# Flamingo block on one core: the first layer's network on sorted tokens instead of on all experts

## The reference, cut to what matters

```python
logits = gelu(xf @ router_w1 + router_b1) @ router_w2 + router_b2
topk_p, topk_i = top_k(softmax(logits), 2)          # shares normalised to 1
v, integrated = 0, xf
for _ in range(2):
    ctx = concat([integrated, v])
    shared_ctrl = gelu(ctx @ shared_w1 + shared_b1) @ shared_w2 + shared_b2
    x_sh, v_sh = inl(shared_ctrl, integrated, v, mu)
    ctrl = expert(ctx, topk_i)                      # its own network for each choice
    x_r, v_r = inl(ctrl, ...) weighted by topk_p and summed over the two choices
    x_next, v_next = sw * (x_sh, v_sh) + (1 - sw) * (x_r, v_r)
    halt = sigmoid(gelu(integrated @ halt_w1 + halt_b1) @ halt_w2 + halt_b2)
    integrated += halt * (x_next - integrated)
    v += halt * (v_next - v)
out = xf + integration_weight * (gelu(integrated @ refine_w1 + b) @ refine_w2 + b)

def inl(ctrl, xs, vs, mu):
    a, b, g = split(ctrl, 3)
    v_next = sigmoid(a) * vs - softplus(b) * (xs - mu)
    return xs + 0.1 * sigmoid(g) * v_next, v_next
```

## Time and profile before

| | us |
|---|---|
| median of 3 runs (lowest to highest) | 648.78 (643.36 to 662.13) |
| the profiled execution | 646.05 |
| its span, first to last instruction | 644.2 |
| mean granted clock of TensorE | 0.928 of full |

### The profile page before, as it was taken

One profiled execution on the slowest core, in us unless ns is written; L12 is line 12 of the kernel. 1 busy time (PEld: TensorE's weight loads), 2 busy tenths in 40 slices (PEclk: granted clock), 3 DMA queues, 4 the chain that ended last, 5 costly groups with the idle time before them and its releaser, 6 DMA issues.

```text
span 644.2 us, 9928 instructions
## 1 busy us (share of the span) xinstructions
PE 572.7 (89%) x3318; PEld 336.9 (52%) x3318; DVE 424.6 (66%) x1054; ACT 308.8 (48%) x630; POOL 203.5 (32%) x214
## 2 busy tenths in 40 slices
PE   4777999999998898999999999998864499999994
PEld 2432344444453343444444444465554499999993
DVE  3897778887277799777335766768757354545445
ACT  2553466666658744554343535455441144444431
POOL 3829301010034360003790500012564623333331
...
GB/s 276 147 197 131 100 187 12 4 2 3 1 193 355 79 1 1 1 0 0 1 130 0 2 14 1 2 0 6 29 35 194 99 214 283 327 327 308 343 211 205
DMA packets 48198, 71.14 MB, mean 110 GB/s; under 512 B 11420, under 2 KB 35300, under 8 KB 47860
## 3 DMA queue, kind: packets, MB, share of 16 engines
...
## 4 chain that ended last, share of the span: by engine, by line
PE 62%; DVE 10%; SPq 10%; DMA 6%; issue 5%; ACT 4%; another core or an unknown queue 2%; POOL 1%; DVEq 0%; ACTq 0%; POOLq 0%
PE psum L1943 18%; PE psum L1758 6%; PE psum L1745 5%; PE psum L1888 5%; PE psum L2219 4%; PE psum L1766 3%; DMA wb<-in_wall_dram 3%; PE psum L1890 3%; PE psum L1722 3%; PE psum L2230 2%; PE psum L1940 2%; SPq L592 2%; DMA stacked<-parts 2%; DMA stacks<-maxT 1%
## 5 line engine op out<-in xcount | busy, mean ns | idle before, releaser
L1943 PE MATMUL psum<-hidden,ew 128*128 128x512 f32 x320 | 145.3, 597 | 0.0
L856 ACT ACTIVATE probs<-psum 128x512 f32<-128x512 f32 x128 | 74.7, 598 | 55.4 <-PE psum L1745 54.9
L1943 PEld LDWEIGHTS psum<-hidden,ew 128*128 128x128 f32 x320 | 61.5, 192 | 69.7 <-issue 68.3
L1136 DVE TENSOR_REDUCE negmax<-psum 128x4 f32<-128x1024 f32 x64 | 76.9, 1211 | 17.8 <-PE psum L1722 17.2
L2219 PE MATMUL psum<-xbT,wb 128*128 128x128 f32 x624 | 79.9, 283 | 1.8 <-DMA wb<-in_wall_dram 1.5
L1652 DVE SCALAR_TENSOR_TENSOR gated<-psum,wb,silu_g 128x128 f32<-128x128 f32 x156 | 43.9, 343 | 55.9 <-ACT silu_g L1056 50.6
L1056 ACT ACTIVATE silu_g<-psum,wb 128x128 f32<-128x128 f32 x156 | 44.6, 370 | 70.6 <-PE psum L2219 52.7
L2219 PEld LDWEIGHTS psum<-xbT,wb 128*128 128x128 f32 x624 | 76.1, 199 | 2.9 <-DMA wb<-in_wall_dram 2.3
L799 POOL DMA_INDIRECT sorted_y<-yb,xb x39 | 37.4, 958 | 80.1 <-DVE yb L1644 80.1
L1745 PE MATMUL psum<-stacks 50*128 50x256 bf16 x256 | 52.6, 298 | 6.2 <-DMA stacks<-maxT 4.0
L2230 PE MATMUL psum<-wb,gated 128*128 128x128 f32 x312 | 42.3, 279 | 8.6 <-DVE gated L1652 8.3
...
## 6 DMA issues: line engine op xcount, KB each, us to landing
...
sorted_x<-in_slots_dram SPq DMA_DIRECT2D x1, 9815.0 KB, 32.7
...
back<-sorted_y SPq DMA_DIRECT2D x4, 512.0 KB, 5.4
...
```

The source lines that it names most:

```text
L856: nc.scalar.activation(probs[:, g % 2, h % 4, :, :], s2[n % 2].rearrange("p (k q) -> p k q", k=2), ACT.Exp, scale=float(HD) ** -0.5).then_ ...
L1136: nc.vector.tensor_reduce(negmax[:, p].rearrange("p h q -> p (h q)"), psum[:, i:i + 2, :].rearrange("p h (q k) -> p (h q) k", q=2), AX.X, ...
L1943: last = nc.tensor.matmul(dst, ew2[:, j, cols], hidden[:, c, k - 1, j, :], start=False, stop=(j == 3))
```

## The change

The first layer's network now computes each expert only for the tokens that chose it. Tokens are sorted in two halves of 1024. A half has 2048 rows (two choices) in regions packed to multiples of 128: 23 blocks (`FIRST_BLOCKS`), each with one expert, whose weights SP loads by a value from `first_table`. All elementwise work is in rows (tokens on partitions). A group is up to four blocks, or one chunk for the shared network; a sub-stage (`subs`) has three routed groups (12 or 11 blocks, `PIECES`), in step 1 with two shared groups ahead of them in every first piece; sub-stage 0 has the four shared groups of step 0. On every engine the sub-stages run in order: `units_of` (transposes, first matmul, gelu), then softplus, then sigmoids, then shares.

States go through DRAM: `scatter_rows` sends normalised tokens to `first_x`, `store_shares` (SP) writes each group's shares, `gather_shares` brings them home by token, `combine` adds them up, `scatter_states` sends the new states to `first_xv` for step 1. `final_columns` turns the last state for `refine_up`. The second layer's chain for chunks 0 and 1 starts after the last group. The masks, their spreading and the columns' state are gone; the constants fall from 25 DMAs to 17. The old functions named in the section above (`hidden_unit`, `spread_choice`, `mask_first`, `controller`, `gate_parts`, `first_step`, `second_step`) and their calls are taken away. `slots` is set, and the new buffers are cleared, by ScalarE's queue within attention (`CLEAR_AT`). `X_BUFS` falls from 10 to 8, and `back` lies over `xp`. The core of the added lines:

```diff
+CLEAR_AT = {(2, 13): "slots", (4, 5): "first_x", (5, 5): "first_xv"}
...
+W_BUFS, X_BUFS = 4, 8
...
+HALVES = 2
+HC = NC // HALVES
+FIRST_BLOCKS = (2 * HC * CH + E * (P - 1)) // P
+HALF_ROWS = FIRST_BLOCKS * P
+FIRST_THRESHOLDS = HC * CH // P
+PIECES = ((0, 12), (12, FIRST_BLOCKS))
+GATHER = 4
+W1_V, W1_OUT, W1_B = HID, 2 * HID, 2 * HID + 3 * D
+W1_COLS = W1_B + 1
+W1_BUFS = 16
+SOFT_BUFS, SIG_BUFS = 3, 4
...
+        add_sub([("shared", 0, c, 4) for c in range(NC)])
+        for it in range(2):
+            for half in range(HALVES):
+                for i, (j0, j1) in enumerate(PIECES):
+                    members = [("shared", 1, HC * half + c, 4) for c in range(HC)] if it and i == 0 else []
+                    add_sub(members + [("routed", it, (half, j), min(GATHER, j1 - j)) for j in range(j0, j1, GATHER)])
...
+            def load_first_rows(it, half, i):
+                j0, j1 = PIECES[i]
+                if it == 0:
+                    sp.wait_ge(rows_out[half], 16 * HC * GR)
+                else:
+                    sp.wait_ge(rows_out[half], 16 * 2 * HC * GR)
+                if it or half:
+                    was = groups_of(*((it, 0) if half else (it - 1, 1)), i)
+                    sp.wait_ge(share_done, was[-1] + 1)
+                if it == 0:
+                    sp.dma_start(xr[:, j0:j1, 1, :], sorted_rows(first_x, half, j0, j1 - j0)).then_inc(rows_in[i], 16)
+                else:
+                    sp.dma_start(xr[:, j0:j1, :, :].rearrange("p j a f -> p j (a f)"),
+                                 sorted_rows(first_xv, half, j0, j1 - j0)).then_inc(rows_in[i], 16)
+            def store_shares(g):
+                _, it, (half, j), n = groups[g]
+                sp.wait_ge(share_done, g + 1)
+                if it == 0:
+                    out_of, dst = rc[:, j:j + n, :, :].rearrange("p j a f -> p j (a f)"), first_c
+                else:
+                    out_of, dst = rc[:, j:j + n, 1, :], first_d
+                sp.dma_start(sorted_rows(dst, half, j, n), out_of).then_inc(shares_out[piece_of(g)], 16)
...
+            def gather_shares(it, c):
+                half = c // HC
+                for i in range(len(PIECES)):
+                    pool.wait_ge(shares_out[i], stored_shares(it, half, i))
+                if it or c >= 2:
+                    pool.wait_ge(combined, NC * it + c - 1)
+                src, n = (first_d, D) if it else (first_c, 2 * D)
+                for t in range(TC):
+                    for k in range(2):
+                        at = 2 * (c * TC + t) + k
+                        nc.gpsimd.indirect_dma_start(brought[:, c % 2, t, k, 0:n], None, src[half],
+                                                     bass.IndirectOffsetOnAxis(ap=slot1[:, at:at + 1], axis=0)).then_inc(home_in[c % 2], 16)
...
+            for half in range(HALVES):
+                for c in range(HC * half, HC * half + HC):
+                    exp_of_gap(c)
+                for c in range(HC * half, HC * half + HC):
+                    scatter_rows(c)
             for c in range(NC):
+                plain_sum(c)
+            for half in range(HALVES):
+                for c in range(HC * half, HC * half + HC):
+                    gather_shares(0, c)
+                for c in range(HC * half, HC * half + HC):
+                    scatter_states(c)
             for c in range(NC):
+                gather_shares(1, c)
+            pool.wait_ge(share_done, len(groups))
             rstd_of_chunk(2, 0)
             rstd_of_chunk(3, 0)
             rstd_of_chunk(2, 1)
...
+            def clear(which):
+                if which == "slots":
+                    act.dma_start(sorted_x.rearrange("(a b) f -> a (b f)", a=16 * (SLOTS // P)),
+                                  a["slots"].rearrange("(a b) f -> a (b f)", a=16 * (SLOTS // P))).then_inc(slots_cleared, 16)
+                    return
+                dst, n = (first_x, D) if which == "first_x" else (first_xv, 2 * D)
+                act.wait_ge(prepared, 1)
+                for half in range(HALVES):
+                    act.dma_start(dst[half].rearrange("(p j) f -> p j f", p=P),
+                                  zeros[:, 0:n].rearrange("p (o f) -> p o f", o=1).to_broadcast([P, FIRST_BLOCKS, n])).then_inc(first_cleared, 16)
...
+            def first_gelus(g):
+                act.wait_ge(up_psum, g + 1)
+                ps = bank[2 + g % 2]
+                if not is_routed[g]:
+                    nc.scalar.activation(shared_h[0:96, groups[g][2], :], ps[0:96, :], ACT.Gelu, bias=sb1[:, 0:1]).then_inc(gelu_done, 1)
+                    return
+                _, _, (_, j), n = groups[g]
+                for i in range(n):
+                    last = nc.scalar.activation(routed_h[0:HID, (j // GATHER) % 3, i * P:(i + 1) * P], ps[0:HID, i * P:(i + 1) * P], ACT.Gelu,
+                                                bias=w1[0:HID, (first_weight(g) + i) % W1_BUFS, W1_B:W1_B + 1])
+                last.then_inc(gelu_done, 1)
...
+            def units_of(sub):
+                for i, g in enumerate(sub):
+                    if g in turned:
+                        keep_turned(g)
+                    if i:
+                        first_gelus(sub[i - 1])
+                first_gelus(sub[-1])
+            def gates_of(sub):
+                nc.scalar.preload_act_table_set("natural_log_exp_and_others")
+                for g in sub:
+                    softplus(g)
+                for g in sub:
+                    sigmoids(g)
...
+            def give_share(g):
+                steps.wait()
+                if not step_of[g]:
+                    nc.vector.scalar_tensor_tensor(x_share(g), v_share(g), DT, gate(g, "g"), ALU.mult, ALU.mult).then_inc(share_done, 1)
+                    return
+                at = groups[g][2]
+                if is_routed[g]:
+                    v = t = tiles_of(xr, g, 0)
+                else:
+                    v, t = xv[:, TC * at:TC * at + TC, 0, :], x_share(g)
+                steps.then(nc.vector.tensor_tensor(t, v, gate(g, "a"), ALU.mult))
+                steps.wait()
+                steps.then(nc.vector.tensor_tensor(t, t, difference(g), ALU.subtract))
+                steps.wait()
+                stored(g)
+                nc.vector.scalar_tensor_tensor(x_share(g), t, DT, gate(g, "g"), ALU.mult, ALU.mult).then_inc(share_done, 1)
...
+            COMBINE_AFTER = {3: (0, 0), 4: (0, 1), 5: (0, 2), 6: (0, 3), 7: (1, 0), 8: (1, 1)}
+            for i, sub in enumerate(subs):
+                if i:
+                    units_of(sub)
+                    softplus_of(sub)
+                    shares_of(sub)
+                if i in COMBINE_AFTER:
+                    combine(*COMBINE_AFTER[i])
...
+            add_refined(0)
+            layer_norm_apply(0, turn(2, 0))
+            maxima2(0)
+            maxima2(1)
+            sums_of(0)
+            fuse(0)
+            fuse(1)
+            third_stats(0)
+            layer_norm_rows(0)
+            add_refined(1)
+            layer_norm_apply(1, turn(2, 1))
+            choose(0)
+            combine(1, 2)
+            maxima2(2)
+            maxima2(3)
+            weights_of(0)
+            slots_of(0)
+            combine(1, L)
...
+            def product(g, part):
+                kind, _, at, n = groups[g]
+                m = products.index((g, part))
+                if m >= 3:
+                    pe.wait_ge(*part_read(m - 3))
+                pe.wait_ge(gelu_done, g + 1)
+                dst = part_bank(m)
+                for i in range(n):
+                    if kind == "shared":
+                        h = shared_h[0:97, at, i * P:(i + 1) * P]
+                        if part == "halt":
+                            last = nc.tensor.matmul(dst[:, i:i + 1], h, sw2[0:97, 3 * D:3 * D + 1], start=True, stop=True)
+                            continue
+                        w = sw2[0:97, 0:3 * D]
+                    else:
+                        h = routed_h[0:HID + 1, (at[1] // GATHER) % 3, i * P:(i + 1) * P]
+                        w = w1[0:HID + 1, (first_weight(g) + i) % W1_BUFS, W1_OUT:W1_OUT + 3 * D]
+                    k = ("a", "soft", "g").index(part)
+                    last = nc.tensor.matmul(dst[:, i * P:(i + 1) * P], h, w[:, k * D:(k + 1) * D], start=True, stop=True)
+                last.then_inc(part_psum, 1)
...
+            def units_of(sub):
+                for i, g in enumerate(sub):
+                    turn_rows(g)
+                    if i:
+                        units(sub[i - 1])
+                units(sub[-1])
+            def products_of(sub):
+                for g, part in products:
+                    if g in sub:
+                        product(g, part)
...
+            pe.wait_ge(share_done, len(groups))
+            final_columns(0)
+            final_columns(1)
+            refine_up(0)
+            refine_down(0)
+            second_columns(0)
+            second_scores(0)
+            second_scores(1)
```

(9 more changed lines are left out.)

1155 lines of the change are left out of this document (546 added, 609 removed).

## The result

| | before | changed |
|---|---|---|
| median, us (lowest to highest) | 655.03 (643.36 to 662.13) | 848.38 (841.98 to 858.36) |
| profiled execution, us (span) | 646.05 (644.2) | 845.41 (843.6) |
| mean granted clock | 0.928 | 0.73 |

The ratio is 1.310, 95% interval 1.288 to 1.332. Both kernels have slower executions at a lower granted clock, and every ratio here compares the faster executions of each (846.2 over 646.1 us in this table), so that it isn't the quotient of the medians; the traces of e3, e4, e5, e9, e12, e17 and e18 are of slower ones. The direction was right; the time lies far above the range, which ended at 738.

A forecast was written before the change was run, and what follows sets the result against it. TensorE alone bounded the first layer's network; afterwards ScalarE's chain and GpSimd's transfers would decide. The first sorted-row scatter would start at 499 instead of 448.5, so 646.05 plus 50.5 us gives 697 us, range 658 to 738.

The forecast's parts named there:

- signs of being wrong: Sub-stages under 13 or over 20 us, early routed transposes, next-layer rstd before 430, or attention ending later than 183.
- The start ... -3: Kernel start: eight fewer constant DMAs and a shorter row-maxima stall save 3 us, between 0 and 4.
- rival D: Attention: clears moved beside the maxima's transfers cost 5 us of waiting in each of three batches, 712 us; chance 0.07.
- Four sub-stages of 15.5: Network, step 0: each sub-stage takes ScalarE 14.7 us plus 0.8 for handoffs; four take the path from 225.5 to 287.5.
- 0.2 more for each ... I take 0: GpSimd's indirect transfers: slowing beside VectorE, at most 26 us at 0.2 each, was taken as 0.
- Shared groups of step 0, the choice of the second half ... hide: Network start: this work and the second half's scatters hide in the first scatters, landing and load, and next sub-stages.
- The landing: After the first sixteen scatters, before the load of rows: 2 us, an estimate.
- Sub-stages of 28 and 21: Network, step 1: 28 us with two shared groups, counted from the routed rows' arrival, 21 without, in each half.
- rival C: Network: TensorE stays at 1.2 GHz after each exchange; step 0's sub-stages grow 5 us, step 1's 12, 757 us; chance 0.10.
- The rule of the Trainium skill: TensorE: small idle times between groups that cycle through PSUM banks make the clock swing.
- Rival E: ScalarE's chain: 27 table loads each stall the engine for as long again, giving 732 us; chance 0.03.

The follow-up runs named there:

- e3: Changed kernel with clears moved late and only the first 16 of 92 weight loads: 806.14 us, ratio 1.235.
- e4: Kernel before, with only the 9.8 MB clear of slots moved into attention on ScalarE's queue: 678.94 us, ratio 1.040.
- e5: e3 plus matmuls without a use ahead of TensorE's waits in the network, to hold the clock: 839.70 us.
- e9: Kernel before plus 32 useless indirect DMAs on GpSimd after the first masks: 675.91 us.
- e12: e10 with only the first 16 of 92 weight loads: 762.40 us.
- e17: e12 repeated unchanged, on the same chip as e18: 755.03 us, ratio 1.163.
- e18: e15 repeated, on the same chip as e17: 749.77 us, ratio 1.158.
- e1: Changed kernel with its clears moved late, first_x after the last maximum, slots and first_xv into the network: 809.71 us, ratio 1.251.
- e6: Changed kernel with its clears still in attention but cut into pieces (slots 24, zeros 18): 805.47 us, ratio 1.244.
- e15: e12 plus matmuls without a use in step 1's waits only: 724.79 us, ratio 1.158.
- e2: Changed kernel with only the first 16 of its 92 weight loads: 823.55 us, ratio 1.265.
- e7: Changed kernel in which each weight load after the 16th brings 8 of 513 columns: 836.35 us, ratio 1.299.
- e10: e6 with the 96 indirect DMAs of gathers and states' scatters replaced by plain DMAs to fixed rows: 795.02 us, ratio 1.227.
- e16: e6 with the sigmoid products of step 0's first two shared groups ahead of the second half's counts on TensorE: 766.91 us, ratio 1.222.
- e8: e6 plus matmuls without a use as in e5, all weight loads kept: 861.82 us.

## Why the prediction was wrong, by its own steps

Two of the signs of being wrong that the prediction named came true: attention ended later than 183 us, and sub-stages took over 20. Failed, in the order of their size: step 0 (+60), step 1 (+49) and attention (+37).

**"The start ... -3" and rival D.** The sum took nothing for the clears, and D had 15 us with a chance of 0.07. D's cause was right and even its waiting was enough: TensorE was idle 10.8 us from 100 to 180 us, 6.5 of them on one maximum that landed after 24.65. (the earlier trace rows had the 32.7 us that the clear takes, and the landing of a transfer issued behind it has to be bounded by that.) What D left out is the lower clock behind a wait, which stood in the earlier trace rows and which I used for the network only. Medians give 39 us (e1) and 43 (e6 against the changed kernel), the ratio of e4 26, and the means of the first scatters 32. The other 5 of the 37 us are, as far as the traces tell, the lower clock from 100 us on, which came without the large clear as well.

**"Four sub-stages of 15.5".** The price of the work was right: 16.7 to 17.9 in e17, 15.6 to 17.1 in e15. What failed is "each queue": I named the weight loads in the change and gave these 92 loads no term, neither their 24 MB nor their place behind `store_shares`. 16 buffers are four groups, a sub-stage is three, so two groups of each sub-stage get weights only after the stores of the one before. Shown: 17 and 15 us (e2, e7), and 22 over three sub-stages beside plain DMAs (e10 against e17).

**"0.2 more for each ... I take 0".** GpSimd's transfers kept their 1.26. What I didn't ask is what they do to others: without loads, sub-stage 4 took 33.5 us beside gathers and scatters and 16.7 beside plain DMAs, on two chips (part of that may be `combine`'s shorter wait; it was not separated). e9 shows it is no tax on a dense stream; and on the chip of e15 and e16 it was absent, with sub-stage 4 at 25.5 in e16, as in e10 without indirect DMAs. ScalarE's copies in e6, then in e16:

```profile
L1028 ACT COPY cols<-psum 128x512 f32<-128x512 f32 x38 | 21.6, 586 | 58.2 <-issue 34.2 <-PE psum L2093 17.4 <-remote 6.5
```

```profile
L1028 ACT COPY cols<-psum 128x512 f32<-128x512 f32 x38 | 21.8, 585 | 55.0 <-PE psum L2093 55.0
```

What holds ScalarE back there stays open. Sub-stages 2 to 4 took 86.0 us, where the forecast had 46.5: 17.7 of the 39.5 go with the loads (e2), 17.0 more with the indirect DMAs (e17 against e2, on another chip), and 4.8 are left. The other 20 us of step 0 are in its first sub-stage.

**"Shared groups of step 0, the choice of the second half ... hide".** They stand ahead of the routed rows on TensorE's queue: 39.5 us from the first scatter to the first routed transposes, not 27.5. The order is 3.7 of it (e16 against e15). The landing, 2 us in the sum with no row behind it, is about 2 more: the last scatter ended at 252.8 us, and SP issued the load at 257.1. The rest differs by chip and was not separated.

**"Sub-stages of 28 and 21" and rival C.** Counted from the arrival of the rows, the first kind took 42.6 us in the first half and 51.2 in the second (506.2 to 557.4), and the second kind took 28.0 and 23.0. The same 64 product records of one first sub-stage took, in the two halves of the changed kernel's own chain:

```profile
442.98 7.27 PE psum L2135 x64
...
514.56 5.14 another core or an unknown queue
...
529.63 0.70 DVE soft L1470
530.36 0.70 DVE shared_c L1475
531.25 0.51 issue
...
542.03 13.86 PE psum L2135 x64
```

The clock was 1.00 in the first and 0.50 in the second. That is C: 1.2 GHz for most of the network (the mean of 0.63 lies near the lower level), where I put 8 us and gave C 0.10. The 51.2 us are 23 over the forecast, and three parts of them can be named. By TensorE's busy time of 21.0 us from 537 to 558 at 0.50, the clock is some 10 us (an estimate), and less in the transposes. Four rounds like the one at 529.63 come 2.1 us apart, at VectorE's pace; the sum had ScalarE's 1.26 us (exp and ln) for each. And from 508.8 to 521 us ScalarE's part of the chain has 10.2 us of waits that the profile gives no cause, 5.14 of them in one piece, beside the second half's gathers until 517 us: the same open effect as in step 0. In the first half, 5 us of `combine` stood on the chain between the two sub-stages, which is the difference between 28.0 and 23.0. The clock's price over all of step 1 was not measured, since holding it cost about what it gave (e18).

The rule of the Trainium skill that the forecast set beside C (page "TensorE: Matmul & The Clock Gate", section "A second HAM failure mode: psum-queue depth-cycling") fits e17 in part, which had small idle times and both levels: TensorE was busy 57.6 of 77 and 62.3 of 77.5 us in the two halves of step 1, at mean clocks of 0.72 and 0.68. The section doesn't say how long the lower clock stays: the changed kernel from 105 to 115 us and e8 from 430 to 450 had 0.50 without any idle time, each behind one wait.

Rival E is refuted: the table loads of the changed kernel's network took 1.28 each, and behind most of them the next operation starts at once (the load at 274.17 us is followed by a gelu at 275.47), as the forecast said. The 9.98 us behind e6's load at 320.14 belong to the open effect above; e16 has the same loads and no such wait.
